# Gated recurrence in a decoder layer: five cumulative-sum products instead of seven, and a new order of the steps of a pair

## What is computed

```
q, k, v = x @ Wq, x @ Wk, x @ Wv          # 16 heads of 16
g = sigmoid(x @ Wf + bf)
state = state * g[..., None] + v[..., None] * k[..., None, :]    # token by token
out_t = einsum('bhij,bhj->bhi', state, q_t)
```

## Time and profile before

| | us |
|---|---|
| median of three runs | 2299.24 (2298.08 to 2299.51) |
| the profiled execution | 2293.58 |
| its span, first to last instruction | 2291.9 |
| mean distance of two pairs in the recurrence, pair 2 to pair 31 | 24.5 |
| distance of two undisturbed pairs | 22.8 |
| TensorE busy, 60 to 780 us | 658.2 of 720 |
| VectorE busy, 60 to 780 us | 533.7 of 720 |
| ScalarE busy, 60 to 780 us | 301.1 of 720 |

### The profile page before, as it was taken

One profiled execution on the slowest core, in us unless ns is written; L12 is line 12 of the kernel. 1 busy time (PEld: TensorE's weight loads), 2 busy tenths in 40 slices (PEclk: granted clock), 3 DMA queues, 4 the chain that ended last, 5 costly groups with the idle time before them and its releaser, 6 DMA issues. The chain is left out here.

```text
span 2291.9 us, 74706 instructions
## 1 busy us (share of the span) xinstructions
PE 2122.2 (93%) x30263; PEld 1440.3 (63%) x30263; DVE 1663.3 (73%) x3010; ACT 1145.6 (50%) x1887; POOL 311.0 (14%) x282
## 2 busy tenths in 40 slices
PE   6989998989989869999999999999899999999698
PEld 4666666666666657777777777776444444444487
DVE  7777776777777757677776767775555558989897
ACT  3444443444444436766667676665211118855365
POOL 5000000000000011111111111111000005445221
PEclk9999999999999979999999999999899999999899
DMA  3010010010000010101101010100000004459674
GB/s 107 21 30 22 25 27 21 23 29 21 26 26 21 21 47 30 42 27 34 35 27 41 27 41 27 41 27 1 1 0 0 0 1 192 192 211 424 233 269 163
DMA packets 78311, 146.48 MB, mean 64 GB/s; under 512 B 10035, under 2 KB 63542, under 8 KB 78134
## 3 DMA queue, kind: packets, MB, share of 16 engines
q1 hardware_dynamic: 78134, 143.70, 17.9%
HBM read 82.84 MB, written 60.82 MB: 63 GB/s over the span
## 5 line engine op out<-in xcount | busy, mean ns | idle before, releaser
L1281 PE MATMUL ff_bank<-ff_xq,w_uh 128*128 (+1 forms) x1536 | 457.8, 380 | 2.8 <-ACT ff_whole L1390 2.8
L1281 PE MATMUL ff_bank<-ff_xq,w_ul 128*128 (+1 forms) x768 | 291.5, 380 | 0.0
L1281 PEld LDWEIGHTS ff_bank<-ff_xq,w_uh 128*128 128x128 f16 x1536 | 149.9, 98 | 181.3 <-issue 4.1
L1595 DVE TENSOR_REDUCE ff_top<-ff_bank 128x512 f32 (+1 forms) x192 | 132.7, 691 | 116.7 <-PE ff_bank L1281 116.7
L465 ACT ACTIVATE x<-rec_e 128x512 f32<-128x512 f32 x192 | 112.0, 596 | 176.9 <-PE rec_e L348 176.9
L1390 ACT ACTIVATE ff_whole<-ff_bank,ff_coef 128x512 int16<-128x512 f32 x192 | 124.5, 682 | 103.5 <-PE ff_bank L1281 46.4
L1062 DVE TENSOR_REDUCE mneg<-att_s 128x4 f32<-128x512 f32 x256 | 158.9, 683 | 21.1 <-PE att_s L819 20.3
L600 DVE TENSOR_TENSOR rec_tmp<-rec_x,x 32x256 f32<-32x256 f32 (+1 forms) x192 | 80.8, 421 | 126.9 <-PE rec_x L385 62.1
L564 DVE TENSOR_TENSOR x<-rec_x,rec_until 128x512 f32<-128x512 f32 x256 | 158.4, 679 | 12.8 <-PE rec_x L332 12.0
L360 PE MATMUL rec_x<-x 32*32 32x64 f32 x8192 | 147.9, 218 | 21.3 <-issue 12.0
L360 PEld LDWEIGHTS rec_x<-x 32*32 32x32 f32 x8192 | 124.6, 106 | 59.3 <-issue 58.8
(11 more groups left out here) (236 smaller groups left out, 4406.9 us busy)
## 6 DMA issues: line engine op xcount, KB each, us to landing
gate_scratch<-ff_out SPq DMA_DIRECT2D x28, 768.0 KB, 3.5
ff_in<-gate_scratch SPq DMA_DIRECT2D x28, 768.0 KB, 11.0
product_scratch<-ff_out SPq DMA_DIRECT2D x28, 768.0 KB, 9.7
ff_out<-product_scratch SPq DMA_DIRECT2D x28, 768.0 KB, 5.9
att_x<-in_x SPq DMA_DIRECT2D x32, 256.0 KB, 2.7
att_ctx<-in_ctx SPq DMA_DIRECT2D x32, 256.0 KB, 2.9
att_o<-rec_scratch SPq DMA_DIRECT2D x32, 256.0 KB, 3.7
out<-s_out SPq DMA_DIRECT2D x16, 512.0 KB, 3.3
```

The lines of the kernel that those rows point to most:

```text
L1281: m = T.matmul(bank_[:], weights(wp, kc, a, c), tile[:, xp, kc], start=(i == 0), stop=(i == len(terms) - 1))
L1595: V.tensor_reduce(top[:, k, bass.ds(n, 1)], banks[k % 6][:], AX.X, ALU.max, apply_absolute_value=True).then_inc(q1["maxed"], 1)
```

## The change

Three kinds of edits, all in the recurrence.

1. **Five exponents instead of seven.** The seven constant matrices become five: inner borders 0 and 2 share one matrix, border 1 and border 3 have one each, and the two outer ones stay. Key and asking factor of a border come from the same sum with opposite signs (`scale` of -1 or 1) and a bias that sends the tokens on the wrong side to zero (`hidden`, now 2x4). ScalarE still makes ten exponentials for each pair: four, two, two, one and one.
2. **The order on TensorE.** value_gate(p, 1) moves from between the two scores to the end of the preceding `pieces`; across for q takes its place between the scores. turn moves ahead of inside 3. The quarter is cut in two halves of 32 products, with value_gate(p + 1, 0) between them. Exponents 0 to 2 stand behind inside 1, 2 and 3, exponents 3 and 4 behind the quarter.
3. **VectorE and ScalarE.** The rounding of n to float16 moves to ScalarE as one more activation (semaphore `h_ready`). On VectorE the two floors come first in a step, then all eight scores_out; weighted(p, 0) of the new pair runs in the same step, between half_out and quarter_out, instead of in the next one between the two scores_out.

TensorE around the two scores, before: value_gate (L309, L311) between them, all of q and half of k (six products) behind.

The diff, cut to what the steps above need (left out: the constants `marks`, `sums_of` and their masks, made once at the start):

```diff
@@ -89,8 +89,10 @@
     NR = 4
     SUB = CH // NR
     FLOOR = -18.0
-    NE = 3 + NR
-    EXPS = NR + NE - 1
+    NE = 5
+    EXPS = 2 * NR + 2
+    USES = (((0, 0), (0, 2), (1, 0), (1, 2)), ((0, 1), (1, 1)), ((0, 3), (1, 3)), ((0, NR),), ((0, NR + 1),))
+    DONE = (4, 6, 8, 9, 10)
...
@@ -337,11 +338,11 @@
                 def exponents(p, s, k):
                     if k == 0:
                         pe.wait_ge(q["consts_ready"], 2)
-                        pe.wait_ge(q["n_ready"], 2 * p + 2)
+                        pe.wait_ge(q["n_ready"], p + 1)
                     if k < 2:
-                        wait_if(pe, q["e_ready"], EXPS * p - (4 if k == 0 else 0))
+                        wait_if(pe, q["e_ready"], EXPS * (p - 1) + DONE[NE - 2 + k])
                     else:
-                        pe.wait_ge(q["e_ready"], EXPS * p + k - 1)
+                        pe.wait_ge(q["e_ready"], EXPS * p + DONE[k - 2])
                     for b in range(2):
                         cols = slice(b * D, (b + 1) * D)
                         for half_ in (nh, nlo):
@@ -374,53 +375,69 @@
                             m = T.matmul(X[0][dst, at], mt[src, b, hd, dst], wa[src, 1, at], start=True, stop=True)
                     m.then_inc(q["o_made"], 1)
 
-                def across_quarter(n):
-                    pe.wait_ge(q["o_taken"], TAKES * n + TAKES + 2)
-                    pe.sem_inc(q["seen"], 1)
-                    for hd in range(H):
+                def across_quarter(n, part):
+                    if part == 0:
+                        pe.wait_ge(q["o_taken"], TAKES * n + TAKES + 2)
+                        pe.sem_inc(q["seen"], 1)
+                    for hd in range(part * HH, (part + 1) * HH):
                         for b in range(2):
                             at = slice(b * D + hd * HD, b * D + (hd + 1) * HD)
                             for chunk in (0, 2):
                                 src, dst = rows(place(b, chunk)), rows(place(b, chunk + 1))
                                 m = T.matmul(X[1][dst, at], mt[src, b, hd, dst], wa[src, 0, at], start=True, stop=True)
-                    m.then_inc(q["o_made"], 1)
+                    if part == 1:
+                        m.then_inc(q["o_made"], 1)
 
                 def products(p, n, s, so, front, back):
                     if back:
                         scores(n, so, 0)
                     if front:
-                        value_gate(p, 1)
+                        across(p, 0, F[1], 0, 0, q["q_made"])
+                        across(p, 0, F[1], 0, 1, q["q_made"])
                     if back:
                         scores(n, so, 1)
                     if front:
-                        across(p, 0, F[1], 0, 0, q["q_made"])
-                        across(p, 0, F[1], 0, 1, q["q_made"])
                         across(p, 1, F[0], 1, 0, q["k_made"])
 
                 def pieces(p, s, before, front, back, more):
                     n, so = p - 1, 1 - s
-                    for i in range(8):
-                        if back:
-                            if i < 4:
-                                inside(n, so, i)
-                            elif i == 4:
-                                across_half(n)
-                            elif i == 5:
-                                across_quarter(n)
-                        if front and i == 0:
-                            across(p, 1, F[0], 1, 1, q["k_made"])
-                        if more and i == 4:
-                            turn(p + 1, so, before + s)
-                        if more and i == 7:
-                            value_gate(p + 1, 0)
-                        if front and i >= 1:
-                            exponents(p, s, i - 1)
+                    if back:
+                        inside(n, so, 0)
+                    if front:
+                        across(p, 1, F[0], 1, 1, q["k_made"])
+                    if back:
+                        inside(n, so, 1)
+                    if front:
+                        exponents(p, s, 0)
+                    if back:
+                        inside(n, so, 2)
+                    if front:
+                        exponents(p, s, 1)
+                    if more:
+                        turn(p + 1, so, before + s)
+                    if back:
+                        inside(n, so, 3)
+                    if front:
+                        exponents(p, s, 2)
+                    if back:
+                        across_half(n)
+                        across_quarter(n, 0)
+                    if more:
+                        value_gate(p + 1, 0)
+                    if back:
...
@@ -451,8 +468,10 @@
                         A.activation(v[:, s, b * D:(b + 1) * D], F[1 - b][:, 0:D], ACT.Copy).then_inc(q["v_ready"], 1)
                     A.activation(ez[:], zc[:], ACT.Exp, scale=-1.0).then_inc(q["ez_ready"], 1)
                     act.wait_ge(q["ez_ready"], p + 1)
-                    wait_if(act, q["n_ready"], 2 * p)
+                    wait_if(act, q["n_ready"], p)
                     A.activation(nl[:], ez[:], ACT.Ln, bias=ones_col[:]).then_inc(q["lg_ready"], 1)
+                    act.wait_ge(q["lg_ready"], p + 1)
+                    A.activation(nh[:], nl[:], ACT.Copy).then_inc(q["h_ready"], 1)
                     act.wait_ge(q["q_made"], p + 1)
                     for m in range(2):
                         A.activation(qm[:, s, :, m], F[1].rearrange("p (k n) -> p k n", k=KC), ACT.Copy,
@@ -460,14 +479,14 @@
                     act.wait_ge(q["k_made"], p + 1)
                     A.activation(kT[:, s].rearrange("p k n -> p (k n)"), F[0][:], ACT.Copy).then_inc(q["k_ready"], 1)
                     act.wait_ge(q["o_taken"], TAKES * p if not isinstance(p, int) or p else TAKES)
-                    for k in range(NE - 1):
+                    for k in range(NE):
                         act.wait_ge(q["e_made"], NE * p + k + 1)
-                        A.activation(e[:, s, k], E[(s + k) % 2][:], ACT.Exp).then_inc(q["e_ready"], 1)
-                        if k == 2 and not (isinstance(p, int) and p == NP - 1):
+                        for asks, r in USES[k]:
+                            out = um[:, s, r] if asks else e[:, s, r]
+                            A.activation(out, E[(s + k) % 2][:], ACT.Exp, bias=hidden[:, asks, r:r + 1] if r < NR else 0.0,
+                                         scale=-1.0 if asks else 1.0).then_inc(q["e_ready"], 1)
+                        if k == 1 and not (isinstance(p, int) and p == NP - 1):
                             turned(p + 1)
-                    act.wait_ge(q["e_made"], NE * p + NE)
-                    for r in range(NR):
-                        A.activation(um[:, s, r], E[s][:], ACT.Exp, bias=hidden[:, r:r + 1]).then_inc(q["e_ready"], 1)
 
                 turned(0)
...
-                            c.did(V.tensor_tensor(sums_of[:, b, r].rearrange("p (c w) -> p c w", c=NC)[:, :, cols],
+                        for k, r, cols in ((0, 0, slice(0, SUB)), (0, 2, slice(2 * SUB, CH)), (1, 1, slice(0, CH)), (2, 3, slice(3 * SUB, CH))):
+                            c.did(V.tensor_tensor(sums_of[:, b, k].rearrange("p (c w) -> p c w", c=NC)[:, :, cols],
                                                   until[:, b].rearrange("p (c w) -> p c w", c=NC)[:, :, cols],
                                                   marks[:, b, r].rearrange("p (c w) -> p c w", c=NC)[:, :, cols], ALU.subtract))
-                        c.did(V.tensor_tensor(sums_of[:, b, NE - 1], marks[:, b, NR], until[:, b], ALU.subtract))
-                        for k, w in ((NR, CH), (NR + 1, 2 * CH)):
+                        for k, r, w in ((3, NR, CH), (4, NR + 1, 2 * CH)):
                             out, all_, border = [x_.rearrange("p (c m w) -> p c m w", m=2, w=w)
-                                                 for x_ in (sums_of[:, b, k], until[:, b], marks[:, b, k + 1])]
+                                                 for x_ in (sums_of[:, b, k], until[:, b], marks[:, b, r])]
                             c.did(V.tensor_tensor(out[:, :, b], all_[:, :, b], border[:, :, b], ALU.subtract))
                             c.did(V.tensor_tensor(out[:, :, 1 - b], border[:, :, 1 - b], all_[:, :, 1 - b], ALU.subtract))
...
@@ -573,15 +594,15 @@
                     V.tensor_scalar(zc[:, b * D:(b + 1) * D], F[1 - b][:, D:], FLOOR, None, ALU.max).then_inc(q["z_ready"], 1)
 
                 def split(p):
-                    dve.wait_ge(q["lg_ready"], p + 1)
+                    dve.wait_ge(q["h_ready"], p + 1)
                     wait_if(dve, q["e_made"], NE * p)
-                    V.tensor_copy(nh[:], nl[:]).then_inc(q["n_ready"], 1)
-                    dve.wait_ge(q["n_ready"], 2 * p + 1)
                     V.tensor_tensor(nlo[:], nl[:], nh[:], ALU.subtract).then_inc(q["n_ready"], 1)
 
                 def weighted(n, s, part):
                     if part == 0:
```

(24 more changed lines are left out.)

47 lines of the change are left out of this document (27 added, 20 removed).

## The result

The changed kernel takes 2314.85 us (median), the kernel before it 2295.18 us on the same chip. The ratio is 1.0084, with a 95% interval from 1.0071 to 1.0097: it is **slower**, by 0.8% or 19 us, where 7 us less was forecast, and 2314.85 lies outside the range of 2272 to 2312. The profiled execution took 2315.55 us (span 2313.8), against 2293.58 (span 2291.9) before.

A forecast was written before the change was run, and what follows sets the result against it. It took a chain through TensorE and VectorE as the bound: +0.40 undisturbed, -0.49 and -0.11 for gaps, -0.20 us a pair, -5.8 over 29; last step -1.6; together -7.4. Median 2299.24 becomes 2292, range 2272 to 2312.

The forecast's parts named there:

- What bounds the kernel: Recurrence: a loop of waits through TensorE and VectorE sets the pair's length, 22.83 us undisturbed, rather than TensorE's total work.
- the undisturbed pair: A recurrence pair without instruction gaps or low clock: 22.83 us before, forecast 23.23 after, 0.40 longer.
- the chain: Loop from last sum through scores_out, TensorE's second scores to quarter, VectorE's quarter_out and total; 22.83 us for each pair.
- the disturbances: Instruction gaps on TensorE (1.09 us for each pair) and half clock (up to 0.5); 1.70 in all over the undisturbed pair.
- TensorE idles for about 1.8 us there, and for another 0.5 ahead of the second scores: "There" is ahead of q, waiting for VectorE's copy of v; 1.8 and 0.5 us of idle time in each pair.
- For the clock I keep 0.5: TensorE at 1.2 GHz costs up to 0.5 us for each pair, as before; the change adds nothing.
- rival: Idling ahead of q halves the clock on q and second scores; with half the pairs 2312 us; chance 0.15.
- 1.09 becomes 0.60, -0.49 for each pair: TensorE's instruction gaps, second scores to quarter, shrink by an assumed factor of 0.55, saving 0.49 us for each pair.
- only the gap at each start of the loop stays (-0.8): Best-case bound on the saving in TensorE's instruction gaps: all vanish but those at loop starts, -0.8 us for each pair.
- -0.11 for the gaps that were beside the chain: Instruction gaps behind the quarter that got through 0.86 us of spare time no longer delay the chain; -0.11 us each pair.
- The start of the small products once more: Restarting the quarter's small products after value_gate splits them costs 0 to 0.3 us for each pair, taken as 0.1.
- the cover of weighted(p, 0): VectorE's 2.28 us between half_out and quarter_out hides behind TensorE's cut quarter with value_gate, by only 0.3 us.

The follow-up runs named there:

- cut: Kernel before with only the quarter cut in two and value_gate(p + 1, 0) between the halves; ratio 1.0304 to the kernel before.
- five: Kernel before with only the five exponents, in the old order on TensorE, VectorE and rounding unchanged; ratio 1.0005 to the kernel before.
- fill16: Changed kernel with 16 large products, results unused, between the first scores and q in each pair; ratio 1.0025 to the kernel before.
- rota: Changed kernel with only TensorE's loop turned, so the jump back lies ahead of the first scores; ratio 1.0036 to the kernel before.
- kfill: Changed kernel, next pair's first floor ahead of quarter_out, all k products ahead of the second scores, eight unused products before inside 0; ratio 0.9997 to kernel before.
- fillpad: fill16 with exponents 1 and 2 made twice over; ratio 1.0086 to the kernel before.
- pad: Kernel before with the products of exponent 3 made three times over, between turn and quarter; ratio 1.0079 to the kernel before.
- rot16: fill16 with TensorE's loop turned, so the jump back lies ahead of the first scores; ratio 0.9950 to the kernel before.

## Why the prediction was wrong

*What bounds the kernel: right for the undisturbed pair.* Its length came out at 23.18 us against 23.23. The floors cost 214.26 - 213.60 = 0.66, and the second scores start 3.11 instead of 2.45 us behind the last sum. A value_gate on the chain costs at least its price (cut). Two exponents fewer, some 0.9 us of TensorE's work in each pair, bring nothing by themselves (five), so TensorE's work is not the bound. But one of the two lay on the chain, and by the chain five should have won 16 us. In the mean pair the disturbances decide.

*"TensorE idles for about 1.8 us there, and for another 0.5 ahead of the second scores": right*, 2.1 and 0.3.

*"For the clock I keep 0.5": this step failed.* The prediction had seen in the earlier trace rows that a stretch in which TensorE is idle for half of the time is followed by one at 0.50, had found that the change makes just such a stretch in every pair, on the chain, and then gave it 0.15 as a rival, because waits of 0.9 us had left PEclk at 0.98. But 0.9 us is not 2.1: cut shows how the same products go from 2.86 to 3.94 us when the wait ahead of them goes from 0.86 to 2.44. The runs showed the clock in two places on the chain. On q it costs +0.70 us for each pair, and fill16, which fills the wait, takes that away. Between the second scores and quarter_out it costs about as much again. Less its gaps, this stretch takes 15.42 - 0.31 = 15.11 us in the 15 pairs whose clock stays up and 18.05 - 1.17 = 16.88 in the 13 others, and only 2 pairs of the kernel before were of that second kind. Over all 28 pairs the stretch less its gaps grew from 15.41 to 15.93 us, though its products alone got 0.24 us shorter: the clock costs 0.76 us more for each pair. That the rival's own number was close (2312 against 2314.85) is in part luck. It put some 0.75 us for each pair on q and the second scores (0.70 on q was measured) and nothing on the rest of the chain, 22 us too little; about as much went the other way, by the relief ahead of the second scores (0.33 us for each pair more than forecast), the first pairs (3.4 us), the stages behind the recurrence (4.6 us) and a median of the kernel before of 2295.18 instead of 2299.24.

*The half clock in the quarter was no step at all.* The cut quarter holds the one group of large products, value_gate, that the clock still falls on, and it has been moved onto the chain for it. From its first to its last record it takes 2.52 us on the mean and 1.98 undisturbed, +0.54 of the +0.76. Before the change it stood beside the chain.

*"1.09 becomes 0.60, -0.49 for each pair": right in direction, a little too large for the chain.* Inside the stretch the gaps fell from 1.10 to 0.71 us for each pair, -0.39, although the stall at the loop's start in it grew from 0.20 to 0.33 for each pair (up to 2.65 us at one jump, for 1.52). The prediction had not counted that stall among its 31.6 us, since it stands in the list of waits under scores_out, and its bound "only the gap at each start of the loop stays (-0.8)" took it as fixed; turning the loop (rota) shows its weight, 0.5% of the time. The products on the chain came out as forecast: the stretch less its gaps, where the clock stays up, went from 15.35 to 15.11, -0.24 for -0.26.

*"-0.11 for the gaps that were beside the chain": too small.* The first column lay 0.44 us above its shortest before (2.89 against 2.45). In the changed kernel the 12 pairs whose q is not slow lie at the shortest, and in fill16 the mean lies 0.07 above. So this relief was 0.37 to 0.44, at least three times as large as forecast; in the changed kernel the clock ate it.

The start of the small products once more (0 to 0.3 us) and the cover of weighted(p, 0): nothing went wrong there. quarter_out starts 0.45 us after VectorE is done with weighted, released by the quarter (L387). ScalarE's rounding holds up nothing that shows: no wait of TensorE in the list is put down to it.

*The Trainium skill*, Runtime: NRT & Kernel Launch (Instruction fetch mechanics), calls the crossing into another block "mostly hidden". In the recurrence it is not, before the change (31.6 us of gaps) or after it (10.7 apart from the jumps).

In sum, for each pair: floors +0.66 as forecast; relief ahead of the second scores -0.44 (forecast -0.11); clock on q +0.70 (forecast 0); stretch to quarter_out +0.08 (forecast -0.75, from -0.26 and -0.49). That is 1.00. Without the last pair the stretch has +0.13: products -0.24, gaps -0.39, clock +0.76. So the clock costs 1.46 us for each pair, some 42 us. By these sums, which are an estimate, the change without it would have been faster by 0.4 to 0.5 us for each pair.

**What stays open:** what brings the half clock onto the value_gate in the quarter. Filling the wait for v did not remove it (fill16), filling another did not either (kfill), the same cut with turn and exponent 3 still ahead of the quarter has hardly any of it (cut), and doubling two exponents lowers the time at 1.2 GHz only from 61 to 48 us (fillpad). Whether gaps for instructions help to bring it down, or only fall into the same pairs (1.17 us of gaps for 0.31), is open too, and so is most of what the median of pad shows above its pairs.

## What to carry to other kernels

A wait on TensorE has two prices: its length, and what it does to the granted clock of the products behind it, so look at what stands behind each wait that a change makes longer, and if that lies on the chain, fill the wait or move it to where nothing depends on what follows. Large products without use in the wait helped at one place here (fill16) and not at another (kfill), so measure them. An operation that is cheap beside the chain can carry disturbances (a low clock, a gap for instructions) that cost nothing there; on the chain they count, so price it with them. A mean over pairs can hide what happened: split the pairs by whether the clock fell in them before you explain it. Put a loop's jump ahead of work that has time to spare, and test parts of a change together as well as apart, since one part may be what makes another possible.

## What the runs showed of the hardware

A wait of 2.1 us ahead of q in each pair was followed by q at 1.2 GHz in 17 of 29 pairs, and one of 2.4 us in cut by slow products in 19 of 29; with waits of 0.9 us none of the products behind was slow. In all there were 28 stretches at 1.2 GHz in 720 us instead of 7. Sixteen products of no use, 1.92 us of them, made the kernel 0.6% faster. In the Trainium skill (TensorE: Matmul & The Clock Gate, Part 1: The HAM clock gate) the clock follows how busy TensorE has been. The traces agree for the waits. TensorE's busy time in the profile does not tell the whole, though: with two exponents of large products fewer between the small ones (five against before) it was busy for 656.1 us of the window instead of 658.2, and the time at 1.2 GHz rose from 31 to 105 us.

In the kernel before, TensorE's gaps for instructions, 0.3 to 1.7 us long, lay a multiple of 256 instructions apart, within 3, in 23 of 27 cases, and in the other four a jump lay between them.

A jump back to the start of a loop of some 6600 instructions held TensorE up by 1.3 to 2.65 us. At inside 0 the mean was 1.4 us (5.7 / 4) before and 2.3 (9.1 / 4) after the change, ahead of the first scores 1.3 in rot16 and 1.8 in rota. What its length depends on is not shown.
